# Block 8 of a deformable bottleneck convolution: its input loaded whole beside the opening's blocks, and its first convolution, pixel and offset work placed before block 0's first tap

## The reference, cut to what matters

```python
out = relu(frozen_bn(conv2d(x, w1)))              # 1x1, 1024 -> 256
offset = conv2d(out, w_off, pad=1) + b_off        # 3x3, 256 -> 18
out = deform_conv3x3(out, offset, w2)             # 9 taps, each read between 4 pixels
out = relu(frozen_bn(out))
x = relu(frozen_bn(conv2d(out, w3)) + x)          # 1x1, 256 -> 1024

out = relu(_gconv(x * m1, w1g)) * m2              # grouped 1x1
out = relu(_gconv(out, w2g)) * m2                 # grouped 3x3
x = relu(_gconv(out, w3g) + x)
```

## Time and profile before

| | |
|---|---|
| runs | 2951.67, 2953.07, 2953.92 us |
| span of the profiled execution | 2953.8 us |
| PE busy | 2809.9 us, 95% |
| DVE busy | 2306.2 us, 78% |
| ACT, POOL busy | 1265.0 us, 1246.2 us |
| last coordinate of block 6 done (end of step 7's work) | 190.45 us |
| first gather | 192.69 us |
| first tap's first matmul | 218.44 us |
| last tap of block 0 done | 278.14 us |

### The profile page before, as it was taken

The page is one execution under the profiler, slowest core; times in us unless marked ns, Lnnn a source line. Parts: engine busy times, 40 slices in busy tenths (PEclk is TensorE's granted clock), DMA queues, the critical chain, the costliest instruction groups (busy, mean ns, idle before and its releaser), DMA issues.

```text
span 2953.8 us, 45116 instructions
## 1 busy us (share of the span) xinstructions
PE 2809.9 (95%) x12064; PEld 1553.2 (53%) x12064; DVE 2306.2 (78%) x5439; ACT 1265.0 (43%) x2530; POOL 1246.2 (42%) x1160
## 2 busy tenths in 40 slices
PE   7969999999999999999999999999999999999998
PEld 3435555555555555455455555555555555555552
DVE  2138888887878878788787878878888898888871
ACT  1224444444444444444444444444444444444442
POOL 2025544434434434344443434444444455555530
PEclk9989999999999999999999999999999999999999
DMA  7679988888888888888888888888888888888862
GB/s 272 201 251 338 318 285 323 319 318 284 302 294 280 322 299 300 288 277 311 297 326 275 301 294 290 313 300 302 310 293 285 288 329 314 319 311 318 325 240 79
DMA packets 263070, 863.50 MB, mean 292 GB/s; under 512 B 31746, under 2 KB 72834, under 8 KB 254336
## 3 DMA queue, kind: packets, MB, share of 16 engines
q0 software_dynamic: 165888, 604.05, 58.1%
q1 hardware_dynamic: 78592, 190.68, 18.9%
q10 hardware_dynamic: 18432, 67.12, 5.6%
HBM read 747.72 MB, written 114.02 MB: 292 GB/s over the span
## 4 chain that ended last, share of the span: by engine, by line
PE 82%; DVE 9%; issue 5%; ACT 1%; DMA 1%; another core or an unknown queue 1%; POOL 1%; DVEq 0%; SPq 0%; ACTq 0%; POOLq 0%
PE psA L413 11%; PE psR L521 11%; PE psD L501 9%; PE psD L503 9%; PE psD L502 9%; PE psR L553 8%; PE psV L482 8%; PE psA L449 4%; DVE val L952 4%; PE psR L534 4%; PE psR L570 4%; PE psR L576 2%; DVE y L935 2%; PE psD L449 1%
## 5 line engine op out<-in xcount | busy, mean ns | idle before, releaser
L378 POOL DMA_INDIRECT corners<-corner_tables,samples_in x1152 | 1230.8, 1068 | 1607.8 <-DVE val L952 1154.1
L952 DVE SCALAR_TENSOR_TENSOR val<-corners,samples_in,val 128x256 f32<-128x256 f32 x3456 | 1417.3, 478 | 77.8 <-ACT val L698 64.3
L712 ACT ACTIVATE valT_hi<-psV 128x512 fp32r<-128x512 f32 x576 | 311.7, 592 | 898.0 <-PE psD L503 694.5
L962 DVE TENSOR_TENSOR valT_lo<-psV,valT_hi 128x512 fp32r<-128x512 f32 x576 | 370.5, 685 | 264.2 <-ACT valT_hi L712 227.3
L521 PE MATMUL psR<-deformed,w_sb 128*128 128x512 f32 x1024 | 485.5, 616 | 46.8 <-DVE y L883 44.7
L698 ACT ACTIVATE val<-corners,samples_in 128x256 f32<-128x256 f32 x1152 | 490.5, 503 | 33.1 <-DMA corners<-corner_tables,samples_in 25.6
L501 PE MATMUL psD<-valT_hi,w_hi 128*128 128x512 f32 x1152 | 484.4, 421 | 0.4 <-DVE valT_lo L962 0.4
L502 PE MATMUL psD<-valT_hi,w_lo 128*128 128x512 f32 x1152 | 456.3, 396 | 0.0
L503 PE MATMUL psD<-valT_lo,w_hi 128*128 128x512 f32 x1152 | 455.9, 396 | 0.0
L482 PEld LDWEIGHTS psV<-const_sb,val 128*128 128x128 f32 x2304 | 264.5, 142 | 192.7 <-issue 131.1
L413 PE MATMUL psA<-x_sb,w_sb 128*128 128x512 f32 x768 | 356.5, 603 | 5.1 <-DMA x_sb<-in_x 5.1
(11 more groups left out here) (78 smaller groups left out, 1571.5 us busy)
## 6 DMA issues: line engine op xcount, KB each, us to landing
y<-in_x SPq DMA_DIRECT2D x128, 512.0 KB
out<-y ACTq DMA_DIRECT2D x128, 512.0 KB
x_sb<-in_x SPq DMA_DIRECT2D x48, 1024.0 KB
corner_tables<-x_sb SPq DMA_DIRECT2D x128, 256.0 KB
corners<-corner_tables,samples_in POOLq DMA_INDIRECT x1152
y<-in_x SPq DMA_DIRECT2D x8, 2048.0 KB, 10.2
corner_tables<-corners SPq DMA_DIRECT2D x8, 1139.0 KB, 5.7
samples_dram<-samples SPq DMA_DIRECT2D x32, 90.0 KB
```

The costliest lines, as they stand in the source:

```text
L378: nc.gpsimd.indirect_dma_start(corners[:, slot, :], None, table, bass.IndirectOffsetOnAxis(ap=index[:, TAPS * t + k:TAPS * t + k + 1], axi ...
L712: nc.scalar.activation(valT_hi[:, m, :], psV[m][:], ACT.Copy).then_inc(valT_ready, 1)
L952: nc.vector.scalar_tensor_tensor(acc, corners[:, n % GS, corner * CMID:(corner + 1) * CMID], samples_in[:, bpar, w:w + 1], acc, ALU.mult, ...
L962: nc.vector.tensor_tensor(valT_lo[:, m, :], psV[m][:], valT_hi[:, m, :].bitcast(F32), ALU.subtract).then_inc(valT_rest, 1)
```

## The change

Block 8's input is loaded whole into `y` like those of blocks 0 to 7, and `conv1` reads it there. In step 8 PE does all of `conv1`, `turn_mid`, `offconv` and `turn_offs` ahead of `turn_val(0)`; ACT does `mid_relu`, `pixels_copy` and `offs_copy` ahead of the first `corner0`; DVE does `halo_mid`, `positions` and `coordinates` ahead of the first `interpolate`. From block 9 on all is as it was.

```diff
-                if low + 1 < LAG_B:
+                if low + 1 <= LAG_B:
                     if low >= 1:
                         sp.wait_ge(conv1_done, 2 * s)
                         sp.sem_inc(sp_waits, 1)
                     sp.dma_start(y[:, 1 - par], x[s + 1]).then_inc(x_early[1 - par], 16)
-                if "A" in on and low >= LAG_B:
+                if "A" in on and low > LAG_B:
                     sp.wait_ge(table_stored, 64 * s)
...
-                if "A" in on and low >= LAG_B:
+                if "A" in on and low > LAG_B:
                     sp.wait_ge(conv1_half, s + 1)
...
-                    if blow < LAG_B:
+                    if blow <= LAG_B:
                         pe.wait_ge(x_early[bpar], 16 * (b // 2 + 1))
                     else:
-                        pe.wait_ge(x_in, 32 * (b - LAG_B) + 16 * (half + 1))
+                        pe.wait_ge(x_in, 32 * (b - LAG_B - 1) + 16 * (half + 1))
...
+                if low == LAG_B:
+
+                    beside = {0: [lambda: conv1(0, 1), lambda: conv1(1, 0), lambda: conv1(1, 1), turn_mid] + each(
+                                  offconv, 0, 1) + [turn_offs],
+                              8: [lambda: conv1(0, 0, ahead=1, chunks=[0])]}
...
                 if low == LAG_B:
+                    for f in each(mid_relu, 0, 1) + each(pixels_copy, 0, 1) + [offs_copy]:
+                        f()
                     corner0(0)
                     corner0(1)
...
+                if low == LAG_B:
+                    before = {}
...
                 if low == LAG_B:
+
+                    for k, f in ((3, halo_mid), (8, positions), (8, coordinates)):
+                        beside[k].remove(f)
+                        f()
                     for c in range(1, 4):
                         interpolate(0, c)
```

More of the change, by code:

```diff
@@ L250, in step @@
                     sp.wait_ge(conv1_done, 2 * s)
-                    if low == LAG_B:
+                    if low == LAG_B + 1:
                         sp.wait_ge(weights_split, N_SPLIT)
@@ L413, in conv1 @@
                         mm = pe.matmul(psA[m][:], w1_sb[:, half * KC // 2 + k, m * P:(m + 1) * P],
-                                       y[:, bpar, half * KC // 2 + k, :] if blow < LAG_B else x_sb[:, k, :],
+                                       y[:, bpar, half * KC // 2 + k, :] if blow <= LAG_B else x_sb[:, k, :],
                                        start=half == k == 0, stop=half == 1 and k == KC // 2 - 1)
```

## The result

The changed kernel takes 2957.78 us, the median of 20 runs (2952.55 to 2960.30), against 2953.04 us for 20 runs of the kernel before on the same chip: a ratio of 1.0016, 95% interval 1.0009 to 1.0023. That is 4.7 us slower, between 2.7 and 6.8 us. It is inside the 0.2% that I called no change, though the interval excludes zero. A second comparison (e7), with 11 runs against 30, gave 2956.87 against 2952.10 us, 1.0018 (1.0009 to 1.0028).

The account below looks back on a forecast made before the run. Up to step 8's first tap everybody waits for transfers and one another; behind it DVE sets the pace. Order gave -1.8 us, one clock fall +2.1 us: +0.3 us, 2954 us forecast; own range 2951 to 2959, widened to 2946.5 to 2961 us.

Parts of the forecast that it names:

- part 1: Block 8's input load: there 13 us before PE wants it, costs nothing; first gather about 5 us sooner, no gain by itself.
- part 2: Step 8 ahead of the first tap: `conv1` to 200.2 us, then the offset chain, leaving DVE free at 214.15 us.
- part 3: First tap of step 8: 24 interpolations take 9.5 us, `valT_low(0)` starts at 223.65 us, `tap(0)` ends at 230.55 us.
- part 4: Between step 8's taps: 13.7 us of PE work gone, DVE paces at 5.95 us per period; sum -1.8 us.
- rival C: Step 8: late gathers still stall DVE once for 1.8 us, 2955.9 us; inside the forecast's 0.68, no chance of its own.
- part 5: PE's clock in step 8: idle times of 2.1 us per period cause one fall, costing +2.1 us.
- rival B: Step 8: the clock falls every other period, four falls, +6.6 us, 2960.4 us; chance 0.17 together with a late load.
- signs of being wrong: Steps 8 and 9: coordinates end well before 214 us, `valT_low` period not 5.95 us, or step 9 onwards loses its distance.
- Rival A: Step 8: PE is the limit after all, so the 13.7 us count in full, -6.1 us, 2947.7 us; chance 0.15.

Follow-up runs that it names:

- e7: The changed kernel itself, compared a second time with the kernel before, and its second profile; 2956.87 against 2952.10 us, 1.0018.
- e4: Changed kernel, but DVE's `positions` and `coordinates` go back to tap 8; 2953.35 us, 1.0006 of the kernel before.
- e5: Changed kernel, but DVE does `positions` and `coordinates` between the interpolations of taps 0 and 1; 2955.89 us, 1.0013 of the kernel before.
- e3: Changed kernel plus four extra matmuls with unread results behind each tap of step 8; 2952.37 us, 1.0004 of the kernel before.
- e10: Changed kernel plus one DVE memset between the interpolations of tap 0 and tap 1; 2955.85 us, 1.0011 of the kernel before.
- e8: Changed kernel plus unread matmuls in step 8, 18 ahead of `turn_val(0)` and 7 behind it; 2949.00 us, 0.9992 of the kernel before.

## Why the prediction was right, by its own steps

**The load** (part 1) cost nothing: `conv1` starts at 185.61 us, right behind step 7's work. The first gather came at 186.99 us, 5.7 us sooner than before.

**What stands ahead of the first tap** (part 2) was forecast to 214.15 us and ended at 213.54 us, in a run whose opening was 0.67 us ahead. e4 shows that this chain is on the path: 3.9 us less of it are 4.3 to 4.9 us less of step 8.

**The first tap** (part 3): `valT_low(0)` forecast 223.65, measured 223.04 us; the end of tap 0 was 229.4 us against 230.55. With the opening's 0.67 us taken off, that is right to 0.1 and 0.5 us.

**What is gone from between the taps** (part 4): here the forecast was short. I let six periods of 5.95 us follow, with the gathers' old delay of 1.8 us gone. Where nothing is late the period is right, as e5 shows (249.55, 255.49, 261.44 us), but the gathers came late again, and worse. This term, put at nothing, measured 4.7 us in the first profile and 1.5 to 2.0 us in the second, where DVE's other waits are for `valT_hi`. It is rival C, which I had priced at 1.8 us and given no chance of its own. Its cause was none that I had considered. I had asked whether the transfers would have room; what was short first was POOL's time to issue them: the gather of tap 3 was held for the rest of a run of DVE instructions that the change itself made twice as long without a pause, by moving `positions` and `coordinates` out in front. Behind that hold the transfers were busy too (a share of 0.91 from 228 to 281 us), so part of the lateness may be the transfers catching up.

**The clock** (part 5): I took one fall at 2.1 us. There were three between the taps in each of the changed kernel's profiles, nearer to rival B. They were not free. Where no late gather covers a fall, the period is 7.00 to 7.04 us instead of 5.95 and DVE waits 1.0 us for `valT_hi`: once in the first profile (257.11 us), and twice in the second, with half a microsecond more in a third period, so 1.1 and some 2.6 us. One fall is worth half of what I priced: I took the price from a fall of 6.8 us at the lower clock (266.3 to 273.2 us before), and those of the changed kernel last 3.4 us each (238.0 to 241.4, 251.6 to 255.0, 265.3 to 268.7 us), for which an estimate by the same sum (half the time lost, 0.6 us hidden) is 3.4 / 2 - 0.6 = 1.1 us. So the number of falls was too low and the price too high, and it is luck that the term of 2.1 us lies between the two measured. I had also placed the limit between 1.80 and 2.79 us of idle time. The clock fell behind 1.98 us at 250.92 us, but idle times of 1.97 to 1.98 us at 250.38, 256.33 and 262.28 us in e5 left it at 1.00, so the length of one idle time does not decide it.

In sum, forecast for step 8: 276.3 + 2.1 - 186.45 = 91.95 us; measured 94.4 and 95.0 us. The moment moved by +2.7 to +3.3 us instead of +0.3 us, within the range. The late gathers and the clock together, less the 2.1 us that I had put in and the 0.5 and 0.2 us by which `valT_low(1)` came sooner than forecast, make up the 3.1 and 2.4 us by which step 8 missed. By its own signs of being wrong the prediction did not hold throughout: the period of `valT_low` was not 5.95 us in most of its six places, and three idle times, not one, were followed by the lower clock. The time came out within the range because the range was wide enough for what it had left out, and that much is luck. A small slip stands in its last sum too: 2954.1 us less 0.7 us is 2953.4 us, not 2954. Rival A is excluded: PE was idle ahead of every `turn_val` but the first, released by `valT_lo`. That everything behind this moment keeps its distance was nearly so in the profiles (2675.7, 2675.8, 2673.5 us), but not between all kernels: the rest varies from 2668.3 to 2677.0 us, and goes with the low clock in it, 46 and 53 us in the two lowest and 66 to 67 in all but one of those above 2674.5, and with PE's idle time in the loop, which is lowest in the same two. The 1.5 to 2 us between the 2.7 to 3.3 us of step 8 and the 4.7 us of the medians must lie there or in the profiles' own scatter, of which the 2.6 us by which the profile of before lies above its median are enough; one profile of before and two of the changed kernel don't tell which. What decides in which order the loop settles, and whether a pass gets a long or a short fall, is open. It is not a change that acts in the loop, since e3 and e8 differ from the changed kernel in step 8 only.

## What to carry to other kernels

Work moved into a hole of the busiest engine is only free if the chain that the hole waits for doesn't pass through it: here the load alone was worth 6 us and `conv1` in the hole perhaps 2 more, while the pixel and offset work, put ahead of the first interpolation, gave all of it back. When an engine's pauses are removed, look for who lived in them: the gather of tap 3 got through where DVE paused or did other work (e5, e10), and was held where it did not. And when filler work takes away a wait, look whether the filler itself stands on the path, as the last four matmuls of e3 did: the sum can stay the same by two effects that cancel. In a profile, an issue instruction that takes six times its usual length beside a transfer share of 0.00 is a held issuer, not a slow memory.

## What the runs showed of the hardware

- An indirect gather that reads its indices from SBUF, the memory in which the interpolations have their inputs, released in the middle of a run of 24 DVE interpolations, took 5.94 us to issue in each of the five profiles that have such a run (two of the changed kernel, e3, e4, e8; 0.94 us is usual) and ended 0.8 us behind that run. It took 1.19 us with one memset of 0.27 us in the middle of the run (e10). Other gathers beside such work took 0.94 us.
- PE's clock fell three times between the taps of step 8, for 3.4 us each. A fall that nothing else covered made the period of a tap 1.05 us longer (7.00 to 7.04 against 5.95 us). Idle times of 1.98 us were followed by a fall in one place and by none in others (e5).
- Matmuls whose result is unused, four behind each tap, kept the clock at 1.00 (2.4 GHz) from 228 to 281 us, and cost 1.7 us where they stood on the path, behind tap 7.
- 25 unused matmuls in PE's idle time, some 2730 us ahead of the end, went with 7.9 us less in the median, of which step 8 holds 1.1 to 1.7 us. The rest goes with shorter falls of the clock and less idle time of PE in the loop (32.9 instead of 40.1 us). That the one causes the other was not shown.
